# Decoder layer on one core: both attentions' weighted sums and denominators made with channels on the partitions

## What is computed

```
x = x + attn(layernorm(x));  x = x + xattn(layernorm(x), ctx);  x = x + experts(layernorm(x))

attn:   alpha = softmax(k @ W0 - |k|^2/2)   over tokens and features together, per head
        N = einsum('bhlf,bhld->bhfd', alpha, v);   D = sum(alpha, over tokens)
        phi = softmax(q @ W0)               over the 64 features
        out = (phi @ N) / (phi @ D + 1e-6);   y = out @ Wo.T + bo
xattn:  weight = softmax(q k^T / sqrt(32))  over the 77 context tokens
        out = weight @ v;                   y = out @ Wo + bo
```

## Time and profile before

| what | value |
|---|---|
| median of 3 runs | 913.57 us (910.67 to 914.4) |
| the profiled execution | 910.57 us |
| its span, first to last instruction | 907.6 us |
| TensorE busy with matmuls | 853.4 us, 94% |
| VectorE busy | 609.5 us, 67% |
| ScalarE busy | 310.1 us, 34% |
| GpSimd busy | 319.6 us, 35% |
| mean granted TensorE clock | 0.998 of 2.4 GHz |

### The profile page before, as it was taken

One profiled execution on the slowest core, in us unless ns is written; L12 is line 12 of the kernel. 1 busy time (PEld: TensorE's weight loads), 2 busy tenths in 40 slices (PEclk: granted clock), 3 DMA queues, 4 the chain that ended last, 5 costly groups with the idle time before them and its releaser, 6 DMA issues.

```text
span 907.6 us, 17162 instructions
## 1 busy us (share of the span) xinstructions
PE 853.4 (94%) x6944; PEld 648.0 (71%) x6944; DVE 609.5 (67%) x894; ACT 310.1 (34%) x510; POOL 319.6 (35%) x307
## 2 busy tenths in 40 slices
PE   5979899999999998989999888999999999998998
PEld 3657678877756543889976675888777556458998
DVE  4767566566555466888868674765764555687887
ACT  3637655210055554111034475641002444440000
POOL 5213312221457888367520032200004745771000
PEclk9999999999999999999999999999999999999999
DMA  8104000424224553255540000012122010316562
GB/s 274 43 26 140 2 1 1 145 74 138 70 70 143 168 193 96 81 190 177 170 139 1 3 3 1 1 55 77 64 92 93 2 26 2 72 45 192 183 193 87
DMA packets 46789, 80.15 MB, mean 88 GB/s; under 512 B 13064, under 2 KB 24104, under 8 KB 46712
## 3 DMA queue, kind: packets, MB, share of 16 engines
q1 hardware_dynamic: 46711, 79.07, 28.3%
HBM read 59.55 MB, written 19.33 MB: 87 GB/s over the span
## 4 chain that ended last, share of the span: by engine, by line
PE 81%; POOL 6%; DVE 5%; ACT 3%; DMA 3%; issue 2%; SPq 0%; POOLq 0%; DVEq 0%; ACTq 0%
PE ps L1238 19%; PE ps L1643 11%; PE ps L1565 6%; PE ps L1649 5%; PE ps L1476 5%; PE ps L1537 5%; PE ps L1246 5%; POOL xT L610 4%; PE ps L1423 3%; PE ps L1500 3%; PE ps L1380 3%; PE ps L1397 3%; PE ps L1280 2%; PE ps L1317 2%; PE ps L1438 2%
## 5 line engine op out<-in xcount | busy, mean ns | idle before, releaser
L610 POOL TENSOR_TENSOR xT<-xT,region 128x1024 f32<-128x1024 f32 (+5 forms) x80 | 129.7, 1622 | 71.1 <-PE ps L1565 65.9
L1643 PE MATMUL ps<-expert_hi,k_hi 128*128 128x256 f32 x512 | 124.6, 283 | 4.6 <-DVE k_hi L1137 4.6
L1153 DVE COPY_PREDICATED region<-region,ps 128x512 f32<-128x512 uint32 x112 | 82.3, 735 | 66.7 <-PE ps L1238 66.0
L1643 PE MATMUL ps<-expert_lo,k_hi 128*128 128x256 f32 x512 | 123.1, 279 | 0.0
L1077 DVE TENSOR_REDUCE region<-ps 128x2 f32<-128x1024 f32 (+2 forms) x96 | 89.1, 954 | 46.2 <-PE ps L1510 25.3
L1238 PE MATMUL ps<-expert_hi,wide_hi 128*128 128x512 f32 x256 | 102.4, 400 | 0.0
L1643 PEld LDWEIGHTS ps<-expert_hi,k_hi 128*128 128x128 f32 x512 | 96.0, 188 | 6.0 <-issue 4.8
L1238 PE MATMUL ps<-expert_hi,wide_lo 128*128 128x512 f32 x256 | 100.0, 391 | 0.0
L1238 PE MATMUL ps<-expert_lo,wide_hi 128*128 128x512 f32 x256 | 99.8, 390 | 0.0
L1643 PEld LDWEIGHTS ps<-expert_lo,k_hi 128*128 128x128 f32 x512 | 96.7, 189 | 0.0
L1137 DVE TENSOR_TENSOR k_hi<-region 128x1024 fp32r<-128x1024 f32 x64 | 81.9, 1280 | 17.1 <-issue 16.8
(11 more groups left out here) (161 smaller groups left out, 1641.5 us busy)
## 6 DMA issues: line engine op xcount, KB each, us to landing
region<-hot_rows SPq DMA_DIRECT2D x128, 128.0 KB, 3.3
expert_hi<-halves_kept SPq DMA_DIRECT2D x22, 384.0 KB, 3.3
expert_lo<-halves_kept SPq DMA_DIRECT2D x22, 384.0 KB, 4.3
halves_kept<-expert_hi SPq DMA_DIRECT2D x16, 512.0 KB, 5.4
halves_kept<-expert_lo SPq DMA_DIRECT2D x16, 512.0 KB, 6.2
expert<-in_value_experts SPq DMA_DIRECT2D x8, 512.0 KB, 4.6
expert<-in_output_experts SPq DMA_DIRECT2D x8, 512.0 KB, 4.4
gb<-scale_rows SPq DMA_DIRECT2D x16, 256.0 KB, 4.0
```

The source lines that it names most:

```text
L610: pool.tensor_tensor(acc(c)[:, heads, lo:CH], acc(c)[:, heads, lo:CH], PT[:, k % RING, heads, lo:CH], ALU.add).then_inc(sem["added"], 1)
L1153: dve.copy_predicated(V3[:, t].rearrange("p (h k) -> p h k", k=HD3), chosen.unsqueeze(2).broadcast_to([P, H3, HD3]), ps[:, n % 4, :].rearr ...
L1643: mm(ps[:, 4 + t // 2, t % 2 * D:(t % 2 + 1) * D], k_hi[n % 2][:, t * P:(t + 1) * P], w[:, slot, columns], start=(n == 0 and t % 2 == 0 an ...
```

## The change

The weighted sums of both attentions are made with channels on the partitions, in quarters of 32, and their denominators are made in the same shape by a second set of products: with `pair_sums[:, 1]` (each key denominator written 16 times side by side) for the linear attention, with a block of ones for the cross attention. VectorE then takes the reciprocal of the whole 128x256 tile of denominators and multiplies, which writes `cxT` at once. The turning back (1431), the transposes of `cx` (1445) and ScalarE's copies `numT` and `cxT` are gone, and so are `vblk` and its twelve DMAs. The transposes of the exponentials (1397) are done on row halves: 16 pieces of 64 tokens, each head of the cross attention by itself. The lags behind 2 become one smaller, and OFFSET becomes (0, 9), so the loop has one step fewer and VALUES_AT becomes 18. The sums alternate between banks 4 and 6.

```diff
@@ layout @@
-        vblk = sb("vblk", [P, B, K2C, WIDE2])
+        v2 = sb("v2", [SKV, B, H2, HD2])
-        rc = sb("rc", [P, 2, H1])
+        rc = sb("rc", [P, D])
+        sums_all = view(2 * PAIRS1 * QUARTER)
+        pair_sums = sums_all.rearrange("p (d k w) -> p d k w", d=2, k=PAIRS1)
+        key_dens = view(PAIRS1)
-        OFFSET = (0, 10)
+        OFFSET = (0, 9)
+        def num_bank(t):
+            return 6 if t % 2 else 4
@@ SyncE: the twelve DMAs to vblk are removed @@
-            for h, r0, r1, c in V2_RUNS:
...
@@ ScalarE @@
-                    if 0 <= (t := s - 2) < TT:
-                        until(act, "numT_ps", b, t + 1)
...
-                        copy(numT.rearrange("p (i s) -> p i s", i=2), ps[:, 4:6, 0:2 * P], "numT_sb")
...
+                        i, used = t % 2, (P, SKV)[a]
+                        turned = phT[:, i, :].rearrange("p (k i s) -> p i k s", i=2, s=HALF)
+                        halves = ps[:, 0:2, :].rearrange("p i (k s) -> p i k s", s=HALF)
+                        copy(turned[0:used], halves[0:used], "fT_sb")
...
-                        copy(cxT[:, t % 2, :, :], ps[:, 4, 0:D].rearrange("p (a s) -> p a s", a=DA), "cxT_sb")
@@ VectorE, step 2 @@
-                    dve.tensor_copy(N1w.rearrange("p k w -> p (k w)"), ps[:, 5, 0:2 * P]).then_inc(sem["n_blk"], 1)
...
+                    dve.tensor_copy(key_dens, turned[:, :, HD1]).then_inc(sem["n_blk"], 1)
+                    for i in range(2):
+                        r = slice(i * HALF, (i + 1) * HALF)
+                        dve.tensor_copy(pair_sums[r, 0, :, i * HD1:(i + 1) * HD1], turned[r, :, 0:HD1])
...
-                        dve.tensor_tensor(N1_dens, N1_dens, ps[:, 6, 0:PAIRS1], ALU.add
-                                          ).then_inc(sem["n_ready"], 1)
-                    for a, t in due(s, 4):
+                        for i in range(2):
+                            r, each = slice(i * HALF, (i + 1) * HALF), [HALF, PAIRS1, HD1]
+                            last = dve.tensor_tensor(pair_sums[r, 1, :, i * HD1:(i + 1) * HD1],
+                                                     key_dens[r].unsqueeze(2).broadcast_to(each),
+                                                     ps[r, 6, 0:PAIRS1].unsqueeze(2).broadcast_to(each), ALU.add)
+                        last.then_inc(sem["n_ready"], 1)
+                    for a, t in due(s, 3):
@@ VectorE, lag 2 @@
-                            step(dve.reciprocal(scale, pairs[:, :, :, HD]))
...
-                        step(dve.reciprocal(rc[:, i, 0:H], num[:, :, HD]))
...
+                        if a * TT + t >= 2:
+                            until(dve, "y_ps", b, a * TT + t - 1)
+                        step(dve.reciprocal(rc[:, :], ps[:, num_bank(t), D:2 * D]))
+                        dve.tensor_tensor(cxT[:, t % 2].rearrange("p a s -> p (a s)"), ps[:, num_bank(t), 0:D],
+                                          rc[:, :], ALU.mult).then_inc(sem["cx_ready"], 1)
@@ TensorE @@
+                def weighted(a, t):
+                    until(pe, "fT_sb", b, a * TT + t + 1)
...
+                    if a * TT + t >= 2:
+                        until(pe, "cx_ready", b, a * TT + t - 1)
+                    for d in range(2):
+                        for k in range((PAIRS1, H2)[a]):
+                            g, quarter = k // TC, slice(k % TC * QUARTER, (k % TC + 1) * QUARTER)
+                            if a == 0:
+                                side_of, turned = pair_sums[:, d, k, :], phT[:, t % 2, PAIR_AT[k] * P:(PAIR_AT[k] + 1) * P]
+                            else:
+                                side_of = ones_f[0:SKV, 0:HD2] if d else v2[:, b, k, :]
+                                turned = phT[0:SKV, t % 2, k * P:(k + 1) * P]
+                            last = mm(ps[quarter, num_bank(t), d * D + g * P:d * D + (g + 1) * P], side_of, turned,
+                                      start=True, stop=True)
+                    last.then_inc(sem["num_ps"], 1)
...
-                        for k in range((PAIRS1, K2C)[a]):
-                            r = P if a == 0 else min(P, K2 - k * P)
-                            last = pe.transpose(ps[0:r, k // TC, k % TC * P:(k % TC + 1) * P],
-                                                phi[:, t % 2, k * P:k * P + r], ident)
+                        r = (P, SKV)[a]
+                        for k in range((PAIRS1, H2)[a]):
+                            for i in range(2):
+                                tokens = slice(i * HALF, (i + 1) * HALF)
+                                last = pe.transpose(ps[0:r, i, k * HALF:(k + 1) * HALF],
+                                                    phi[tokens, t % 2, k * r:(k + 1) * r], ident[tokens, tokens])
...
-                    for a, t in due(s, 4):
-                        until(pe, "cxT_sb", b, a * TT + t + 1)
+                    for a, t in due(s, 3):
+                        until(pe, "cx_ready", b, a * TT + t + 1)
```

More of the change, by code:

```diff
@@ L39, in decoder_layer @@
     DCP, SKV = d["ctxT"].shape[0], d["ctxT"].shape[2] // B
-    V2W = HD2 + 1
     K2 = H2 * SKV
-    K2C = -(-K2 // P)
-    K2L = K2 - (K2C - 1) * P
-    FIRST2 = [c * P // SKV for c in range(K2C)]
-    HEADS2 = [(min((c + 1) * P, K2) - 1) // SKV + 1 - FIRST2[c] for c in range(K2C)]
-    WIDE2 = max(HEADS2) * V2W
     SCALE2 = float(HD2) ** -0.5
@@ L241, in decoder_layer @@
         PIECES = 2 * E3
-        V2_RUNS = [(h, max(h * SKV, c * P), min((h + 1) * SKV, (c + 1) * P), c)
-                   for c in range(K2C) for h in range(FIRST2[c], FIRST2[c] + HEADS2[c])]
         FIRST_OF = [sum(TC * (k + 1) for k in range(c)) for c in range(NC)]
@@ L1347, in gates @@
                     last.then_inc(sem["gate_ps"], 1)
-                def sums_turned(t):
-                    until(pe, "fT_sb", b, t + 1)
-                    if t == 0:
+                def weighted(a, t):
+                    until(pe, "fT_sb", b, a * TT + t + 1)
+                    if a + t == 0:
                         until(pe, "n_ready", b, 1)
-                    else:
-                        until(pe, "numT_sb", b, t)
-                        until(pe, "cxT_sb", b, t - 1)
-                        until(pe, "xT_ready", b, TT + max(0, t - 4))
-                    for k in range(PAIRS1):
-                        g, quarter = k // TC, slice(k % TC * QUARTER, (k % TC + 1) * QUARTER)
-                        for i in range(2):
-                            r = slice(i * HALF, (i + 1) * HALF)
-                            last = mm(ps[quarter, 4 + i, g * P:(g + 1) * P], N1w[r, k, :],
-                                      phT[r, t % 2, PAIR_AT[k] * P:(PAIR_AT[k] + 1) * P], start=True, stop=True)
-                    last.then_inc(sem["numT_ps"], 1)
+                    if a * TT + t >= 2:
+                        until(pe, "cx_ready", b, a * TT + t - 1)
[10 more added lines that the diff above has]
+                    last.then_inc(sem["num_ps"], 1)
                 for s in range(LAST):
@@ L1383, in _ @@
                         last.then_inc(sem["f_ps"], 1)
-                    if 3 <= s < TT + 2:
-                        sums_turned(s - 2)
+                    for a, t in due(s, 2):
+                        if a + t:
+                            weighted(a, t)
                     if s == 2:
@@ L1425, in _ @@
                         last.then_inc(sem["y_ps"], 1)
-                    for a, t in due(s, 2):
-                        if a == 0:
-                            until(pe, "numT_sb", b, t + 1)
-                            until(pe, "cx_ready", b, t)
-                            for k in range(TC):
-                                last = pe.transpose(ps[:, 6, k * P:(k + 1) * P], numT[:, k * P:(k + 1) * P], ident)
-                            last.then_inc(sem["num_ps"], 1)
-                            continue
-                        until(pe, "fT_sb", b, a * TT + t + 1)
-                        until(pe, "cx_ready", b, a * TT + t)
-                        for k in range(K2C):
-                            w0, w, r = FIRST2[k] * V2W, HEADS2[k] * V2W, min(P, K2 - k * P)
-                            last = mm(ps[:, 6, w0:w0 + w], phT[0:r, t % 2, k * P:(k + 1) * P], vblk[0:r, b, k, 0:w],
-                                      start=(k == 0), stop=(k == K2C - 1), skip_group_check=True)
-                        last.then_inc(sem["num_ps"], 1)
-                    for a, t in due(s, 3):
-                        until(pe, "cx_ready", b, a * TT + t + 1)
-                        until(pe, "cxT_sb", b, a * TT + t)
-                        for h in range(DA):
-                            last = pe.transpose(ps[:, 4, h * P:(h + 1) * P], cx[:, t % 2, h * P:(h + 1) * P], ident)
-                        last.then_inc(sem["cxT_ps"], 1)
-                    for a, t in due(s, 6):
+                    for a, t in due(s, 5):
                         norm_transpose(b, a + 1, t)
```

78 lines of the change are left out of this document (17 added, 61 removed).

## The result

| | median | runs | span of the profiled run |
|---|---|---|---|
| before | 912.18 us | 4 | 907.6 us |
| the change | **940.0 us** | 4 (933.92 to 948.08) | 946.3 us |

The ratio is **1.0276**, 95% interval 1.0236 to 1.0316: slower, by about 25 us. The ratio leaves out the run of 948.08 us, which counts as slow because it lies over 1.5% above the shortest. The forecast was 934 us, range 926 to 946.

A forecast was written before the change was run, and what follows sets the result against it. VectorE, nearly full inside the steady steps, was to set them once the reciprocals widened. Batch 0's +9.8 and batch 1's +10.8 give +20.6 us on 910.57, so 931.2, predicted as a median of 934 us, range 926 to 946.

The forecast's parts named there:

- The chain for batch 0: Walk through batch 0's steps in us of the old profile: last residual sum at 154.8 against 146.41, +8.4 us.
- The reciprocal: VectorE, 16 times a batch: widened to 256 columns, taken at 1.753 us, adding 1.52 (linear) or 1.55 us (cross) a step.
- The low bound of 0.98: Lower bound in us for the 256-column reciprocal on VectorE, from two short PSUM forms at 3.1 ns a column.
- VectorE's steps: Steady steps on VectorE: linear 4.07 + 1.53 = 5.60 us, cross 3.20 + 1.54 = 4.74 us.
- the first rival: VectorE's idle time swallows the reciprocals and the lighter TensorE sets the step: 902 us, chance 0.03.
- TensorE hidden: TensorE's linear step comes to about 4.7 us, under VectorE's 5.60, so its savings are priced at nothing.
- third rival: TensorE sets the step after all, half transposes at the high bound: 5.8 linear, 5.4 cross; 946 us, chance 0.10.
- Step 2: One copy to `N1w` becomes three, one addition becomes two: 0.6 us on the path, between 0.2 and 1.0.
- The sum per batch: Whole kernel: batch 0 costs 9.8 us more and batch 1 10.8 us more, together +20.6 us.
- the 1.4 of values behind batch 0: After batch 0's last residual sum, one more tile of values lies behind it on TensorE: 1.4 us more work.
- the fourth rival: Granted clock falls to 1.2 GHz because TensorE waits 1 us in most steps: 990 us, chance 0.02.
- After the loop nothing was given back: After the last residual sum TensorE is dense in both kernels, so the delay stays in full.

The follow-up runs named there:

- e10_fill2: The change plus unread 256-column products on TensorE where it waits longest (steps 2, 8, 10, 17, 18): 932.96 us, ratio 1.0246.
- e9_again: The change once more, unaltered, to see time and granted clock together: 934.14 us, ratio 1.0243.
- e11_again: The change once more, unaltered, on one chip beside e10_fill2: 948.62 us, ratio 1.0395.

## Why the prediction was right, and where it was short

The direction and the mechanism, VectorE's reciprocal in the steady steps, were right; the forecast of 934 us fits the runs without a fall of the clock. That the median of the result, 940.0, lay inside the range is in part luck, as the last point but one says. The chain for batch 0, mark by mark, is best read against e10_fill2, whose clock was full, since the sum had assumed that:

| mark in batch 0, us | forecast | clock full (e10_fill2) | the change, clock 0.970 |
|---|---|---|---|
| step 3 starts | 70.6 | 71.4 | 70.4 |
| five steps end | 98.6 | 99.2 | 98.9 |
| step 8, residual sum | 99.9 | 100.9 | 101.2 |
| first cross maximum | 105.9 | 106.8 | 109.0 |
| step 13's maximum | 125.1 | 126.5 | 134.1 |
| last residual sum | 154.8 | 157.0 | 164.5 |

The last row of each in VectorE's timeline, e10_fill2 and then the change, against 146.41 before:

```profile
156.95 0.42 DVE L1005 TENSOR_TENSOR X<-ps,X 128x256 f32<-128x256 f32 x1 [0.89 <-PE ps L1407]
```

```profile
164.51 0.42 DVE L1005 TENSOR_TENSOR X<-ps,X 128x256 f32<-128x256 f32 x1 [0.89 <-PE ps L1392]
```

- **The reciprocal** at 1.753: measured 1.739. The low bound of 0.98, drawn from 8 and 16 columns, was far off: from 128 to 256 columns it is (1.739 - 0.938) / 128 = 6.3 ns a column, twice the 3.1 of the short forms. The larger form in SBUF was the right neighbour. The estimate of 2.13 us from the Trainium skill (VectorE: DVE Perf Modes, the walkthrough of the 8-slice pipeline), which rests on the repeat count of 8, is 22% above what every run shows. By that page's 0.96 GHz the measured slope would be 6 cycles a column, again as an estimate.
- **VectorE's steps** at 5.60 and 4.74: measured 5.58 to 5.59 and 4.66 (140.01 to 144.67). The cross step was 0.08 too high; why stays open. The old steps were read too short: 4.23 us is step 5 alone against a mean of 4.60, and the cross step of 3.49 is 3.58 from maximum to maximum. So VectorE's margin was some 0.5 us in a linear step and 0.4 in a cross step, more than the 0.2 to 0.4 of the first rival, and a linear step grew by 1.0 us rather than 1.4. The sum goes by marks of the timeline and not by these steps, so it is not touched.
- **TensorE hidden** at 4.7 us. Its full-height sums took 1.08 us (forecast 1.00; 0.67 to 0.68 at 64 rows), the halves 0.71 (forecast 1.1), so about 4.4 in all, under 5.58. The third rival's condition never arose in steps at full clock. It did arise at 1.2 GHz: from 116 to 127 us TensorE is busy without a gap, and the cross step there takes 5.05 us (117.38 to 122.43), against 3.67 in e10_fill2 (114.63 to 118.30). The row-group rule of the Trainium skill (TensorE: Matmul & The Clock Gate, on row and column tiling) goes with the trace as to the sums, 1.08 against 0.68, and the halves go with its other side: pairs in different row groups cost 0.71 for 16 where eight full-height ones before took 1.09. No run here separates this rule from other reasons.
- **Step 2** at 0.6: step 3 starts at 70.42 against a forecast of 70.6, which is in part luck. Step 2's own maximum came 0.63 us earlier than before (63.34 for 63.97); from it to step 3's the change takes 7.08 us, where the forecast had 70.6 - 63.97 = 6.6.
- **The sum per batch.** At full clock the last residual sum of batch 0 is 156.95 - 146.41 = +10.5 later (forecast +8.4), and that of batch 1 is at 613.47 against 590.87 before, so +12.1 between the two (forecast +10.8, with the 1.4 of values behind batch 0 and without those behind batch 1). The kernel is 22.3 us over the old one's median of that series, 910.68; the forecast was 20.6. So VectorE's part was right within 2 us a batch. A small part is the filler's own: in step 8 the residual sum comes 7.20 us behind step 7's maximum, against 6.88 in e9_again without filler. In step 2 it costs nothing that shows (6.94 us from maximum to maximum); e10_fill2 comes to step 3 later than the change's profile (71.4 for 70.4) because its step 2 already began later (64.41 for 63.34).
- **The step that failed is the fourth rival's price and chance.** I had argued that the clock would stay at 1.00, because TensorE had waited 8.4 of 52 us before without leaving it, and priced only an all-out fall in the steady steps: 990 us, chance 0.02. The steady linear steps did keep 1.00, with TensorE busy for 70%. The fall came in part: in step 2, at the projections and steps 11 and 12 between them, and at the end of the loop. Mean clocks of the change were 0.966 to 0.991, and its runs went up to 21 us over the 933. Such a partial fall should have been a case of its own, with some tenths of the chance, and with its price: TensorE's work on the path around the two projections, doubled, which the passages show to be 7 to 9 us a batch. The range had room for it only because it had been stretched to the third rival's 946; e11_again's median lies outside. The Trainium skill (TensorE: Matmul & The Clock Gate, "A second HAM failure mode") tells of short idle times between groups of matmuls that make the clock swing between its two levels; the falls at 1.2 to 1.8 us of waiting and e10_fill2 agree with it, the steady steps, which waited 1.20 us each at 1.00, do not, and I had not weighed it.
- **After the loop nothing was given back**, as forecast: e10_fill2's span is 23.6 us over the old one's, of which 22.6 had come up by 613.47.

How large is the fall? At two levels, a mean of 0.970 over 946.3 us stands for about 2 x 0.030 x 946.3 = 57 us at 1.2 GHz. Of these, 2 x 0.25 x (40.76 + 40.80) = 41 us lie in the two passages, where TensorE's work would have been 20 us shorter at full clock. The two profiled runs differ by 15.1 us (948.08 and 932.96), and their passages by 40.76 + 40.80 - 2 x 32.84 = 15.9. So the passages hold the whole difference between these two. The change's runs at 0.989 to 0.991 need hardly more time (933.03 to 934.14 us) than e10_fill2 at 0.998, so the 8.4 us for each 0.01 hold only below 0.99; that these runs had both passages at full clock would fit, but none of them was profiled.

## What to carry to other kernels

Before work is moved to an engine, look for its margin inside the steady step and not over a stretch: here VectorE had 32 us idle, and 0.2 to 0.6 us a step where it mattered. Replacing a narrow division by one spread over the whole tile costs the width in full, and a saving on another engine's transposes pays only while that engine sets the step: taken alone into the old kernel, the half transposes gave 0.4%. An engine that loses the bound also starts to wait, and on TensorE waits like the 1.2 to 1.8 us here, ahead of work on the path, can cost two thirds as much again through the granted clock (15.7 us on top of 22.3). Read PEclk in short stretches, compare the same stretch in both batches, and try useless products there as a test.

## What was unexpected of the hardware

- The clock fell after single waits of 1.2 to 1.8 us at the projections, yet stood at 1.00 through five steps with 1.2 + 0.24 us of waiting each. In one execution the same instructions behind the same waits ran at a mean of 0.79 in batch 0 and at 1.00 in batch 1.
- Once down, it stayed at 1.2 GHz for some 13 us with TensorE busy nearly all the time.
- The same program got mean clocks from 0.966 to 0.991, and a filler of 23 products a batch raised them to 0.996 to 0.998.
- A power of -1 on GpSimd costs 41.1 us for 128x256 fp32 values.
